# Two attention outputs divided on GpSimd and projected from padded head rows, batch 0 inside the attention stage

## What is computed

```python
# layer 0: 16 heads of width 8, full softmax; top-1 mixture of 8 experts (128 -> 512 -> 128)
attn = softmax(einsum('bqhd,bkhd->bhqk', q, k) / d ** 0.5)
out  = einsum('bhqk,bkhd->bqhd', attn, v).reshape(b, n, d) @ Wo.T + bo
# layer 1: 16 heads of width 8, causal softmax with a bias by distance; top-2 mixture of 8 experts (128 -> 128 -> 128)
att = where(causal, q @ k.T / sqrt(D) + rel_bias, -inf); y = softmax(att) @ v
out = y.reshape(B, T, C) @ W_proj + b_proj
# layer 2: linear attention, FP4-quantised MLP; layer 3: gated linear attention (x + ... , then LayerNorm)
```

## Time and profile before

| | |
|---|---|
| runs | 1136.69, 1140.49, 1141.01 us |
| profiled execution | 1136.72 us, span 1134.9 us |
| TensorE / VectorE / ScalarE / GpSimd busy | 933.7 / 821.1 / 621.7 / 137.1 us |
| mean granted TensorE clock | 0.908 |
| layer 0: attention, experts and projection | 50 to 422.5 us, 429.1 to 502.4 us |
| layer 1: attention, projection, experts | 540 to 849.3 us, 850.1 to 868.4 us, 869.2 to 940 us |

### The profile page before, as it was taken

The page is one execution under the profiler, slowest core; times in us unless marked ns, Lnnn a source line. Parts: engine busy times, 40 slices in busy tenths (PEclk is TensorE's granted clock), DMA queues, the critical chain, the costliest instruction groups (busy, mean ns, idle before and its releaser), DMA issues. The chain is left out here.

```text
span 1134.9 us, 22212 instructions
## 1 busy us (share of the span) xinstructions
PE 933.7 (82%) x8663; PEld 482.4 (43%) x8663; DVE 821.1 (72%) x1538; ACT 621.7 (55%) x1318; POOL 137.1 (12%) x146
## 2 busy tenths in 40 slices
PE   5289999999899968945699999999888996676598
PEld 4112222222222217933245444454437775644468
DVE  6597999999899804555676777666726668899587
ACT  4307888888788873425046666665661335333362
POOL 3006300000000144720000000000000001111122
PEclk9658999999999998977579999999998997889699
DMA  4645513304403043826703233332100000000001
GB/s 139 181 82 124 132 39 96 95 3 97 96 1 97 31 102 117 257 75 222 155 22 86 51 72 77 78 86 64 29 1 2 5 1 1 1 1 1 3 6 33
DMA packets 60537, 78.26 MB, mean 69 GB/s; under 512 B 18696, under 2 KB 44065, under 8 KB 60386
## 3 DMA queue, kind: packets, MB, share of 16 engines
q1 hardware_dynamic: 52482, 52.87, 18.8%
q0 software_dynamic: 6896, 23.07, 6.9%
q10 hardware_dynamic: 1056, 0.91, 0.3%
HBM read 51.37 MB, written 17.90 MB: 61 GB/s over the span
## 5 line engine op out<-in xcount | busy, mean ns | idle before, releaser
L780 DVE TENSOR_REDUCE a_negmax<-a_mbank 128x1 f32<-128x1024 f32 (+7 forms) x512 | 485.9, 987 | 110.9 <-PE a_mbank L615 76.7
L746 ACT ACTIVATE a_probs<-a_ebank 128x512 f32<-128x512 f32 (+3 forms) x896 | 432.9, 554 | 216.1 <-PE a_ebank L645 106.2
L608 PE MATMUL a_mbank<-a_moving,a_still 48*128 48x512 bf16 (+4 forms) x1280 | 274.7, 382 | 55.0 <-DVE a_negmax L780 21.3
L636 PE MATMUL a_ebank<-b_moving,b_still 50*128 50x512 bf16 (+4 forms) x1280 | 269.5, 360 | 28.9 <-ACT a_probs L746 25.0
L659 PE MATMUL a_acc<-a_probs,a_slot_v 128*32 128x512 f32 (+3 forms) x1792 | 221.1, 566 | 0.7 <-ACT a_probs L746 0.7
L636 PEld LDWEIGHTS a_ebank<-b_moving,b_still 58*64 58x64 bf16 (+1 forms) x1280 | 84.1, 101 | 220.3 <-ACT a_probs L746 175.6
L608 PEld LDWEIGHTS a_mbank<-a_moving,a_still 56*64 56x64 bf16 (+1 forms) x1280 | 69.1, 104 | 176.1 <-DVE a_negmax L780 110.2
L645 PE MATMUL a_ebank<-a_bias_b,anti 64*64 64x176 bf16 (+4 forms) x1728 | 96.7, 228 | 0.0
L645 PEld LDWEIGHTS a_ebank<-a_bias_b,anti 64*64 64x64 bf16 x1728 | 68.2, 108 | 7.5 <-issue 0.5
L615 PE MATMUL a_mbank<-a_bias_a,anti 64*64 64x176 bf16 (+3 forms) x576 | 65.2, 242 | 0.0
L1599 POOL TENSOR_TENSOR f_xb<-x,b_row 128x512 f32<-128x512 f32 x4 | 4.9, 1258 | 438.1 <-SPq L1293 438.1
(11 more groups left out here) (359 smaller groups left out, 1131.8 us busy)
## 6 DMA issues: line engine op xcount, KB each, us to landing
a_slot_v<-vo SPq DMA_DIRECT2D x16, 512.0 KB, 5.3
stack<-s_parts SPq DMA_DIRECT2D x16, 384.0 KB
b_moving<-stack SPq DMA_DIRECT2D x64, 96.0 KB, 3.5
b_still<-stack SPq DMA_DIRECT2D x32, 192.0 KB, 4.2
a_still<-stack SPq DMA_DIRECT2D x62, 96.0 KB, 2.6
a_moving<-stack SPq DMA_DIRECT2D x62, 96.0 KB, 2.6
stack<-s_parts SPq DMA_DIRECT2D x16, 256.0 KB
a_bias_b<-trow SPq DMA_DIRECT2D x32, 66.0 KB, 4.2
```

The source lines that it names most:

```text
L608: last = nc.tensor.matmul(mbank[COLS * c:COLS * (c + 1), bank, lo:hi], S.a_still[rows, pr, at[c]:at[c] + COLS], S.a_moving[rows, pr, lo:hi ...
L636: last = nc.tensor.matmul(ebank[COLS * c:COLS * (c + 1), s % NE, lo:512], S.b_still[rows, buf, pr, at:at + COLS], S.b_moving[rows, buf, h, ...
L746: nc.scalar.activation(probs[:, g % 2, j, lows[g]:512], ebank[:, s % NE, lows[g]:512], ACT.Exp).then_inc(p_full, 1)
L780: nc.vector.tensor_reduce(negmax[:, qt // HTILES, at:at + 1], mbank[:, use % 2, 0:(qt + 1) * P if causal else SEQ], AX.X, ALU.max, negate= ...
```

## The change

1. `project_phase` and the `project` steps of `experts_and_projection` (transposes, reciprocal, product, transpose, copy) are removed. A tile of 128 tokens is now projected by `project_tile`: four accumulating float32 matmuls that read `S.vo` as it stands against weights padded to 32 rows a head (`S.heads_out`, zero rows for sums and padding).
2. Before that the head rows are divided by their sums. Per quad: gather the four rows of sums into 128 x 32 (`gather_sums`, a DMA), `reciprocal` on VectorE (`invert`), a DMA to DRAM, a DMA back that repeats each row over 32 partitions (128 x 1024, 512 KB), and a GpSimd product over 128 x 1024 (`divide_heads`). Quads 0 to 6 are done by GpSimd's stream in the attention stage; quad 7 in the stage after, its DMAs on SyncE.
3. VectorE inverts quads 0 to 4 inside the first pass, quads 5 and 6 after all its other work of the stage, and adds the eight tiles of batch 0 after that.
4. TensorE projects batch 0's eight tiles in `first_pass` slots of the last quad, every second slot in layer 0 and every fourth in layer 1. From tile 2 on each waits until tile t - 2 has been added.
5. Batch 1's tiles come in `experts_and_projection` at blocks 9, 12, 15, 18 and after the last block, and in `moe_phase` four each behind pairs 10 and 13.
6. GpSimd adds the projection's bias to all of `S.x` in the attention stage. In layer 0 it clears and sorts the rows right after the loads, no longer behind the expert fetches; the fetches now go between the quads' divisions.

```diff
+def project_tile(nc, S, layer, t, out):
+
+    BQ = HEADS // QUAD
+    for q in range(BQ):
+        last = nc.tensor.matmul(out, S.vo[:, t // BT * BQ + q, t % BT * P:(t % BT + 1) * P],
+                                S.heads_out[:, layer, q, :], start=q == 0, stop=q == BQ - 1)
+    return last
...
+def gather_sums(eng, S, q, sums):
+
+    return eng.dma_start(sums[:], S.vo[HD:P:VW, q, :].rearrange("j (k c) -> j k c", c=VW))
+
+
+def store_inverses(eng, S, inverse):
+
+    return eng.dma_start(S.inverse_dram.rearrange("(p c) -> p c", c=VW), inverse[:])
+
+
+def load_inverses(eng, S, inverses):
+
+    return eng.dma_start(inverses[:], bass.AP(S.inverse_dram.tensor, 0, [[SEQ, QUAD], [0, VW], [1, SEQ]]))
+
+
+def divide_heads(nc, S, q, inverses):
+
+    return nc.gpsimd.tensor_tensor(S.vo[:, q, :], S.vo[:, q, :], inverses[:], ALU.mult)
+
...
+    layer = 1 if causal else 0
+    tiles_from = NQUAD * USES + (2 if sort else 1)
+    tile_every = (starts[0] - (tiles_from - NQUAD * USES)) // BT
...
-                pool.dma_start(mask32[:], S.tile_masks).then_inc(masks_loaded, 16)
+                pool.dma_start(mask32, S.tile_masks).then_inc(masks_loaded, 16)
                 pool.wait_ge(masks_loaded, 16)
-                nc.gpsimd.tensor_copy(mask16[:], mask32[:]).then_inc(masks_ready, 1)
-                pool.wait_ge(m_full, 2 * USES)
+                nc.gpsimd.tensor_copy(mask16[:], mask32).then_inc(masks_ready, 1)
                 pool.dma_start(S.sorted_dram, S.empty_rows).then_inc(rows_cleared, 16)
-                for b in range(AHEAD):
-                    pool.wait_ge(m_full, (2 * b + 6) * USES // 2)
-                    fetch_expert(nc, S, b).then_inc(expert_loaded, 16)
                 pool.wait_ge(rows_cleared, 16)
                 for t in range(NT):
                     nc.gpsimd.indirect_dma_start(
@@ -572,10 +605,25 @@
                         in_=S.xr[:, t, :], in_offset=None).then_inc(rows_sorted, 16)
                 pool.wait_ge(rows_sorted, 16 * NT)
                 pool.dma_start(S.sorted[:], S.sorted_dram.rearrange("(b p) c -> p b c", p=P)).then_inc(sorted_loaded, 16)
+            if loads:
+                pool.wait_ge(late_loaded, 16 * len(loads))
+            nc.gpsimd.tensor_tensor(S.x[:], S.x[:], S.b_row[:, layer, :].unsqueeze(1).to_broadcast([P, NT, P]), ALU.add
+                                    ).then_inc(biased, 1)
+            for q in range(NQUAD - 1):
+                pool.wait_ge(acc_empty, 2 * q + 3)
+                gather_sums(pool, S, q, sums).then_inc(sums_loaded, 16)
+                if sort and q < AHEAD:
+                    fetch_expert(nc, S, q).then_inc(expert_loaded, 16)
+                pool.wait_ge(inverted, q + 1)
+                store_inverses(pool, S, inverse).then_inc(inverse_stored, 16)
+                pool.wait_ge(inverse_stored, 16 * (q + 1))
+                load_inverses(pool, S, inverses).then_inc(inverses_loaded, 16)
+                pool.wait_ge(inverses_loaded, 16 * (q + 1))
+                divide_heads(nc, S, q, inverses).then_inc(divided, 1)
+                pool.wait_ge(divided, q + 1)
+            if sort:
                 pool.wait_ge(sorted_loaded, 16)
                 pool.wait_ge(expert_loaded, 16 * AHEAD)
-            if loads:
-                pool.wait_ge(late_loaded, 16 * len(loads))
...
+                    elif n >= tiles_from and (n - tiles_from) % tile_every == 0 and (n - tiles_from) // tile_every < BT:
+                        projected((n - tiles_from) // tile_every)
+                        yield
+
+            def projected(t):
+
+                n = tiles_from + t
+                pe.wait_ge(m_empty, NQUAD * USES + max(t + 2, NM + 1))
+                if sort and t == 0:
+                    pe.wait_ge(bias_parts, 6)
+                pe.wait_ge(divided, BATCH * 2)
+                project_tile(nc, S, layer, t, mbank[:, n % NM, 0:P]).then_inc(m_full, 1)
 
...
+            def invert(q):
+                dve.wait_ge(sums_loaded, 16 * (q + 1))
+                nc.vector.reciprocal(inverse[:], sums[:]).then_inc(inverted, 1)
+
             def quad(q, loaded, earlier):
                 for use, what in enumerate(uses):
+                    if use == LATE + 2 and q >= 3:
+                        invert(q - 3)
                     index = q * USES + (use + 1)
...
+            for q in range(NQUAD - 3, NQUAD - 1):
+                invert(q)
             dve.wait_ge(biased, 1)
...
+            for t in range(BT):
+                n = tiles_from + t
+                dve.wait_ge(m_full, n + 1)
+                nc.vector.tensor_tensor(S.x[:, t, :], mbank[:, n % NM, 0:P], S.x[:, t, :], ALU.add).then_inc(m_empty, 1)
+            dve.wait_ge(m_empty, NM + NQUAD * USES + 1 + BT)
+
...
+    BETWEEN = [9, 12, 15, 18]
...
+                if i >= 2:
+                    pe.wait_ge(added, i - 1)
+                if i == 0:
+                    pe.wait_ge(divided, 1)
+                project_tile(nc, S, 0, BT + i, pr[:, i % 2, 0:P]).then_inc(product, 1)
...
+                if b in BETWEEN:
+                    project(BETWEEN.index(b))
...
+            for i in range(CT, BT):
+                project(i)
...
+            pool.wait_ge(inverses_loaded, 16)
+            divide_heads(nc, S, NQUAD - 1, inverses).then_inc(divided, 1)
             pool.wait_ge(tokens_ready, 1)
...
-            sp.wait_ge(o_turned, NT)
+            gather_sums(sp, S, NQUAD - 1, sums).then_inc(sums_loaded, 16)
+            sp.wait_ge(inverted, 1)
+            store_inverses(sp, S, inverse).then_inc(inverse_stored, 16)
+            sp.wait_ge(inverse_stored, 16)
+            load_inverses(sp, S, inverses).then_inc(inverses_loaded, 16)
             for i in range(3):
...
+                if i in PROJECT:
+                    project(PROJECT.index(i))
...
```

More of the change, by code:

```diff
@@ L1071, in _ @@
             take(1)
+            dve.wait_ge(sums_loaded, 16)
+            nc.vector.reciprocal(inverse[:], sums[:]).then_inc(inverted, 1)
             for b in range(NB):
@@ L1074, in _ @@
                     take(b + 2)
-                if b == AFTER - 1:
-                    nc.vector.tensor_tensor(xb[:], S.x[:], bias.unsqueeze(1).to_broadcast([P, NT, P]),
-                                            ALU.add).then_inc(biased, 1)
-                    dve.wait_ge(biased, 1)
-                if b >= AFTER:
-                    project(b - AFTER)
+                if b in BETWEEN:
+                    project(BETWEEN.index(b))
                 result(b)
-            dve.wait_ge(added, NT)
+            for i in range(CT, BT):
+                project(i)
+            dve.wait_ge(added, BT)
             for i in range(4):
@@ L1130, in moe_phase @@
         hid = sb("hid", [P, 2, CH])
+        sums, inverse = (sb(n, [P, VW]) for n in ("sums", "inverse"))
+        inverses = sb("inverses", [P, SEQ])
         gp = ctx.enter_context(nc.psum_tensor(f"{name}_gp", [P, 512], F32))
@@ L1173, in second_bias, with project @@
                 last.then_inc(b_full, 1)
+            def project(k):
+                if k:
+                    pe.wait_ge(projected, k)
+                else:
+                    pe.wait_ge(divided, 1)
+                for t in range(CT):
+                    last = project_tile(nc, S, 1, BT + CT * k + t, pr[:, t * P:(t + 1) * P])
+                last.then_inc(product, 1)
             hidden(0)
@@ L1239, in _ @@
                     last.then_inc(added, 1)
+                if i in PROJECT:
+                    k = PROJECT.index(i)
+                    part = S.x[:, BT + CT * k:BT + CT * (k + 1), :]
+                    dve.wait_ge(product, k + 1)
+                    nc.vector.tensor_tensor(part, part, pr[:].rearrange("p (t c) -> p t c", c=P), ALU.add
+                                            ).then_inc(projected, 1)
                 if e == E - 1:
```

196 lines of the change are left out of this document (50 added, 146 removed).

## The result

The changed kernel takes 1183.24 us, the median of four runs (1178.4 to 1184.47), against 1138.99 for the kernel before: 1.038 times as long, 95% interval 1.034 to 1.043. Every ratio here leaves out the executions that took over 1.5% more than the fastest one of the same kernel. It was forecast slower, at 1171 us in a range from 1153 to 1188; its profiled execution took 1178.4 us (span 1176.6) where the sum gave 1169.7. The next sections ask why the sum was 8.7 us short.

What follows compares the result with a forecast made beforehand. It saw no engine with slack in layer 0's quads, ScalarE and TensorE pacing the last quad, and layer 1's projection stage running alone. Terms summed to +33.0 us, 1169.7 from the profiled execution or 1173.5 from the median; predicted 1171, range 1153 to 1188.

Steps and rivals of the forecast that it cites:

- The chain in front of tile 2: Last quads: serial chain from quad 5's reciprocal to tile 0's addition, 15.0 us; stalls cost +14.5 and +21.4 us.
- The load of the inverses: 512 KB broadcast load within the chain: 6.1 us from GpSimd's queue, 5.3 from SyncE's.
- Rival (c): Both attentions and experts' start: broadcast load or GpSimd's product takes 5 us longer, total 1186 us; chance 14%.
- Tiles and clock: Last quads: tiles 2 to 7 cost +3.5 and +4.2 us, half clock after the stall +2 each.
- layer 1's last quad: Layer 1's attention end: stall +21.4, tiles +4.2, clock +2; +27.6 us in all.
- The sort: Crossing from layer 0's attention to its experts: sorting earlier shortens the gap from 6.6 to 0.8 us, -5.8.
- Layer 0's quads: Layer 0's attention up to VectorE's last split: +1.9 us, for reciprocals counted in full.
- the five reciprocals: Inside each layer's quads on VectorE: 5 x 0.38 = 1.9 us, full in layer 0, half in layer 1.
- Experts of layer 0: Layer 0's experts phase: GpSimd's issues keep their 2.56 us pace, first store at 12.3 us; 0, bounds -3 and +6.
- project_phase: Layer 1's separate projection stage, 850.12 to 869.21, disappears: -19.1 us.
- moe_phase: Phase with eight of batch 1's tiles: tiles +8.5, gate matmuls may save 1; +7.5 us.
- layer 0's last quad: Layer 0's attention end: stall +14.5, tiles +3.5, clock +2; +20.0 us in all.

Runs made afterwards that it cites:

- e1: Changed kernel with the reciprocal of quad 5 moved from behind VectorE's last work into the last quad's first pass: 1177.53 us, 1.008 times before.
- e6: Changed kernel without batch 0's eight tiles in either attention (no projection matmuls or additions there; gathers, reciprocals, divisions stay): 1175.7 us, 1.007 times before.
- e8: Changed kernel with the inverses' load reading 4 by 32 different rows by the same three-step address: 1182.32 us in a single execution.
- e9: Changed kernel with each load of the inverses made as four loads, one per row, each read by 32 partitions: 1194.94 us, 1.020 times before.
- e5: Kernel before with scatters and sorted load directly behind the clearing at quad 2, ahead of the six expert fetches: 1161.17 us, 0.990 times before.
- e11: Kernel before with only the clearing of the sorted rows issued earlier, ahead of GpSimd's wait for quad 2: 1172.71 us, 1.0049 times before.
- after: The changed kernel unaltered, as first timed and traced: median 1183.24 us, 1.038 times before; its profiled execution took 1178.4 us.
- e4: Changed kernel with GpSimd's wait and product for quad 7 moved behind the fetch of block 3 in the experts phase: 1174.14 us, 1.032 times before.
- e3: Changed kernel with the clearing of the sorted rows put back behind the wait for the second quad: 1202.75 us, 1.028 times before.
- c0: The changed kernel run once more, unaltered, on one chip beside variants and the kernel before: 1182.06 us, 1.033 times before.
- e2: Changed kernel with the inverses' load reading 128 different rows of expert weights by a simpler address: 1192.1 us, 1.021 times before.
- e10: Changed kernel with e1, e3, e4, e9 together, first tiles' additions around layer 1's FP4 work, `bias_parts` wait one tile later: 1159.74 us, 0.992 times before.

## Why the prediction was right, and where its terms were off

1. **The chain in front of tile 2**: right in both layers, step by step, with its start behind VectorE's last table work and behind the FP4 work. e1 and e6 show that it is the cause. Its length was put at 15.0 us and measured 17.4 (402.58 to 420.01) and 16.4 (855.92 to 872.31). TensorE's waits, 10.92 and 19.11 us, are shorter than the 14 and 21 that were to be looked for: tiles 0 and 1 took time ahead of them, in layer 0 with the wait for `bias_parts` and the half clock, which the prediction had not foreseen there. The chain sets when tile 2 starts, so this does not change the sum.
2. **The load of the inverses**: put at 6.1, measured 8.2 to 8.6. This is the mis-sized term of the chain; store (2.0 to 2.9), product (2.33 for 2.4) and gather (2.1 to 2.4) held. Rival (c) had named the broadcast load as the doubtful part, but for its repeated reading; e8 and e9 show that the form of the address, with its four-long outermost step, was at fault.
3. **Tiles and clock**: in layer 0 a tile takes the group from 2.39 to 2.94 us, 0.55 for the 0.6 forecast. The granted clock was at its lower level for tile 2 in both layers (eight matmuls in 2.08 us, where 1.16 is the full-clock figure), as forecast, though in layer 0 it had fallen before the stall. Tile 2 started 16.9 and 22.7 us late, for the 14.5 and 21.4 forecast; tiles 2 to 7 and the clock, put at 5.5 and 6.2 us together, came to 5.1 and 3.9. So layer 1's last quad came out 1.0 us under its forecast for all that its chain was longer by 1.4.
4. **The sort**: -5.7 for -5.8 in the pair of traces from the first chip. No run shows it alone, since e5 was run where the crossing was short already (e11), and in after the last copy comes 26.9 us later, so that a late sort might have been hidden as well. What I left out is what its clearing does at its new place. I had moved the transfer and costed only its end, not the loads it is now beside. Layer 0's quads were 3.0 us over their forecast: after was 1.9 us late at ScalarE's first copy (110 us), before the clearing, 6.1 at its third (158 us) and 4.9 at the last split. So the clearing is worth some 4 us there, and part is made up again, although the five reciprocals, put at 1.9, come in that stretch (e11, held against the same trace, goes from 0.8 to 4.9 us late between these two copies).
5. **Experts of layer 0**: put at 0, measured +2.6. The first store came 14.0 us after the stage's start and not 12.3: the load of the inverses took 7.6 us from SyncE's queue and not 5.3, the steps before it 0.7 us less than put. By e4 most of a late first store counts. From the start of the first store to that of the last it took 52.2 us where the forecast had 51.5, and its own figures had left 0.3 that was called 0. With the 1.7 of the first store that is 2.7. The issues 2.56 us apart held, and the 2.97 us store is gone.
6. **project_phase** -19.1 for -19.1. **moe_phase** +8.6 for +7.5: the saving on the gate matmuls did not come (6.11 us in after for 5.07, at a granted clock of 0.58 in those 6 us where before has 0.73 in its first 5); the rest of the phase took 7.6 us more, where 8.5 was put for the tiles.

So the sum missed 8.7 us: 3.0 in layer 0's quads (the clearing), 2.6 by the experts, 2.0 in layer 0's last quad, 1.1 in moe_phase, 1.0 in small ones, less the 1.0 of layer 1's last quad.

## What to carry to other kernels

When work moves to an idle engine, write down the serial chain from the last thing that releases it to the first thing that waits for it, DMA latencies included: here one reciprocal's place in VectorE's stream was worth some 25 us (e1 against e3), with the same work on GpSimd. And where a consumer's own inputs are ready (tile 0's addition needed nothing of quads 5 and 6), don't put it behind work that waits. A bulk transfer that is moved has to be costed at its new place against the small loads there. And before a load takes its price from a row of the same size, count the engines it can use; when a change bundles several moves, try the free one alone, and trace the unaltered kernel on the chip where it is tried: the early sort came out at 0.99 or 0.996 of before, and without that trace its cause can't be told.

## What the runs showed of the hardware

- One DMA of 512 KB whose address is 4 by 32 by 1024 shows the signs of four of sixteen DMA engines (4 small packets, two tenths busy): 7.6 to 9.0 us from issue to product in layer 0 of after and c0. As 128 rows of one step it shows those of sixteen (16 small packets, nine tenths busy): 3.4 to 4.3 us in layer 0 of e2. As four DMAs of 32 rows it took 6.5 us in layer 0's last quad, with GpSimd's four issues of 0.50 us in it. In layer 1's first five quads, beside its other transfers, the first form took 12.8 to 15.9 us and the second 4.0 to 6.4; only GpSimd waited for those.
- Reading one DRAM row 32 times costs nothing that can be seen beside that (9.1 us in e8 with distinct rows, 9.0 in c0, on one chip).
- The same program took 1138 to 1139 us on two occasions and 1166 to 1169 on two other chips. The experts phase of the kernel before, 73.3 us in the earlier trace rows's execution, took 83.4 and 83.6 us in e11 and e5: there GpSimd's issues are not unbroken (from the first store to the last fetch it waits 11.0 us for `m_y` in e11, never over 0.3 at a time in before), and an edit's worth can change with that.
- In every trace from the two slower chips ScalarE, and TensorE with it, pauses in layer 0's attention for no wait that the profile shows (it says "issue" or "remote"): the longest is 3.6 to 8.5 us and ends between 148 and 169 us in e1, e2, e3, e5, e6, e9 and e10, and is 10.8 us from 402 in e11. None of the six traces from the other two chips has such a pause of over 1.5 us there. What it is stays open.
